# Routed experts: the gathered rows split first and turned by a transposing DMA, instead of turned by TensorE and split after

## The reference

```
H     = einsum('btd,od->bto', x, W) + adapter term        # c, the layer's output
sh    = sum_e gelu(c @ Wsh_up[e]) @ Wsh_down[e]           # 2 shared experts
probs = softmax(c @ W_router)                             # 16 experts, top 2
rt    = sum_e gate[:, e] * (gelu(c @ Wrt_up[e]) @ Wrt_down[e])
out   = x + sh + rt
```

## Time and profile before

| | us |
|---|---|
| median of three runs | 678.12 |
| span of the profiled execution | 642.9 |
| its own total | not given apart; median less span is 35.2 |
| PE busy, share of the span | 620.6, 97% |
| DVE, ACT, POOL busy | 427.3, 323.5, 169.7 |
| share of the 16 DMA engines by the SP queue / POOL queue | 40.7% / 20.9% |
| PE in the chain that ended last | 87% |
| L1405 (x transposes, 316 matmuls) in that chain | 5% |

### The profile page before, as it was taken

How to read it: one execution, slowest core, us unless ns; L and a number is a source line. 1 busy time by engine, 2 the same in 40 slices (tenths; PEclk the granted TensorE clock), 3 DMA queues, 4 the chain that set the end, 5 groups by cost and what they waited for, 6 DMA issues and landing times.

```text
span 642.9 us, 13313 instructions
## 1 busy us (share of the span) xinstructions
PE 620.6 (97%) x4116; PEld 430.5 (67%) x4117; DVE 427.3 (66%) x820; ACT 323.5 (50%) x487; POOL 169.7 (26%) x254
## 2 busy tenths in 40 slices
PE   4999999999999999989999999999999999999995
PEld 2566666666666677567777777777777777766662
DVE  2769989999888983355555555555555553688986
ACT  0256467676784522335555555555555554334340
POOL 0000000000001002233333333333333305777750
PEclk8999999999999999989999999999999999999999
DMA  6699974343235233385555555555555538999977
GB/s 277 258 377 422 421 274 164 130 163 132 105 116 203 102 131 126 112 303 164 163 160 160 158 158 163 155 162 161 161 161 163 163 114 296 342 311 388 397 278 245
DMA packets 49477, 135.62 MB, mean 211 GB/s; under 512 B 6000, under 2 KB 6000, under 8 KB 47024
## 3 DMA queue, kind: packets, MB, share of 16 engines
q1 hardware_dynamic: 38016, 97.86, 40.7%
q0 software_dynamic: 11440, 37.50, 20.9%
HBM read 86.31 MB, written 49.02 MB: 211 GB/s over the span
## 4 chain that ended last, share of the span: by engine, by line
PE 87%; DVE 6%; DMA 3%; ACT 1%; issue 1%; SPq 0%; POOL 0%; DVEq 0%; ACTq 0%; POOLq 0%
PE bank L1440 16%; PE bank L1421 16%; PE bank L1272 12%; PE bank L1349 11%; PE bank L1362 10%; PE bank L1405 5%; PE bank L1280 4%; PE bank L1297 4%; PE bank L1261 3%; PE bank L1430 3%; PE bank L1288 2%; PE bank L1335 1%; DMA region<-w_r 1%; DMA rtw<-x_rows 1%; DVE rtw L906 1%
## 5 line engine op out<-in xcount | busy, mean ns | idle before, releaser
L1149 DVE SCALAR_TENSOR_TENSOR region<-bank,scale,region 128x512 f16<-128x512 f32 x79 | 59.3, 750 | 114.3 <-ACT region L786 114.3
L1440 PE MATMUL bank<-rtw,tmp 128*128 x474 | 116.4, 382 | 2.8 <-DVE tmp L1157 2.8
L1421 PE MATMUL bank<-rtw,region 128*128 x948 | 116.7, 273 | 0.0
L1421 PEld LDWEIGHTS bank<-rtw,region 128*128 128x128 f16 x948 | 93.0, 98 | 10.3
L564 POOL DMA_INDIRECT region<-xc_dram,slot_idx x79 | 78.0, 988 | 61.3 <-POOL slot_idx L561 61.3
L1362 PE MATMUL bank<-shw,hid 128*128 128x512 f16 x384 | 86.2, 379 | 1.9 <-DVE rtw L1216 1.5
L1349 PE MATMUL bank<-act_in,shw 128*128 128x256 f16 x768 | 87.6, 273 | 0.1
L793 ACT ACTIVATE region<-bank,un_dn 128x512 f32<-128x512 f32 x79 | 54.3, 688 | 58.9 <-PE bank L1440 58.1
L1349 PEld LDWEIGHTS bank<-act_in,shw 128*128 128x128 f16 x768 | 75.0, 98 | 12.7 <-issue 0.6
L584 POOL DMA_INDIRECT rtw<-r_dram,pos x64 | 66.1, 1033 | 42.6 <-issue 37.1
L1440 PEld LDWEIGHTS bank<-rtw,tmp 128*128 128x128 f16 x474 | 46.6, 98 | 41.9 <-issue 4.2
(11 more groups left out here) (159 smaller groups left out, 829.4 us busy)
## 6 DMA issues: line engine op xcount, KB each, us to landing
r_dram<-region SPq DMA_DIRECT2D x79, 256.0 KB, 3.3
rtw<-rt_w SPq DMA_DIRECT2D x16, 1024.0 KB, 11.4
act_in<-xT SPq DMA_DIRECT2D x16, 512.0 KB, 4.3
xc_dram<-rows SPq DMA_DIRECT2D x16, 512.0 KB, 3.4
xcT_dram<-hid SPq DMA_DIRECT2D x16, 512.0 KB, 2.9
rtw<-x_rows SPq DMA_DIRECT2D x16, 512.0 KB, 5.5
rtw<-xcT_dram SPq DMA_DIRECT2D x10, 512.0 KB, 5.6
out<-rtw SPq DMA_DIRECT2D x9, 512.0 KB, 5.5
```

Source lines behind the costliest of these rows:

```text
L1149: nc.vector.scalar_tensor_tensor(xgT[s][:, 1], R_XT[s][:].rearrange("p (k t) -> p k t", k=HK), col(scale, C_ALL).bitcast(F32), xgT[s][:, 0 ...
L1421: last = mm(R_UP[s][:, 0:D], xgT[s][:, xp, k, :], rtw[:, bass.ds(e, 1), w0:w0 + D].rearrange("p a d -> p (a d)"), start=(k == 0 and n == 0 ...
L1440: last = mm(R_DN[s][:], midT[s][:, xp, m, :], rtw[:, bass.ds(e, 1), w0:w0 + H].rearrange("p a h -> p (a h)"), start=(m == 0 and n == 0), s ...
```

## The change

The x rows are split before they are turned. Each gathered tile stays in rows: ACT writes its high half and DVE its low half from `xg` into `xh[r]`, a [128, 2 x 512] float16 tile, and SP issues one `dma_start_transpose` that turns the 128 x 1024 numbers from SBUF into `xgT[r]`, [128, 8 x 128], also in SBUF. PE has no transposes of x any more, and the two PSUM banks of `R_XT` are unused in this stage. `xg`, `xh` and `xgT` become rings of three (`RING`), with `xh[2]` in the memory of `xam` and `xgT` and `rrow[1]` in that of `hid`. x is prepared three tiles ahead instead of two. All loops of the stage take six tiles (`TURN`), and what stands outside them is written out.

```diff
-        routed_bufs = carve([((H,), F32), ((2, HK, P), F16), ((H,), F32)] * 2)
-        xg, xgT, rrow = routed_bufs[0::3], routed_bufs[1::3], routed_bufs[2::3]
+        routed_bufs = carve([((H,), F32)] * RING + [((2, H), F16)] * 2 + [((H,), F32)])
+        xg = routed_bufs[0:RING]
+        xh = routed_bufs[RING:RING + 2] + [xam_both[:].bitcast(F16).rearrange("p (a h) -> p a h", a=2)]
...
+        def turn(i, m):
+            return TURN * i + m, m % RING, 2 * i + m // RING
@@ sync
+            def transpose_x(i, m, done=None):
+                j, r, n = turn(i, m)
+                if isinstance(i, int) and j < RING:
+                    sp.wait_ge(down_ready, NT * EARLY - NT if m < 2 else NT * EARLY)
+                sp.wait_ge(sorted_ready, 1)
+                if isinstance(i, int) and j < FIRST:
+                    sp.wait_ge(xh_first, j + 1)
+                else:
+                    sp.wait_ge(xh_ready, done)
+                sp.dma_start_transpose(xgT[r].rearrange("p a k t -> p (a k) t"),
+                                       xh[r].rearrange("p a h -> p (a h)")).then_inc(xgT_loaded[r], 16)
...
+            def move_step(i, m):
+                j = TURN * i + m
+                if not (isinstance(i, int) and j == 0):
+                    store_r(j - 1, (m - 1) % 2)
+                transpose_x(i + (m + RING) // TURN, (m + RING) % TURN, j)
@@ gpsimd, gather
-                if not first:
-                    pool.wait_ge(xgT_psum, j - 1)
+                if not first:
+                    pool.wait_ge(xh_ready, j - RING - FIRST + 1)
+                elif j >= RING:
+                    pool.wait_ge(xh_first, j - RING + 1)
@@ scalar
-            def r_high(j, s):
-                act.wait_ge(xgT_psum, j + 1)
-                nc.scalar.activation(xgT[s][:, 0], R_XT[s][:].rearrange("p (k t) -> p k t", k=HK), ACT.Copy,
-                                     scale=col(scale, C_ALL).bitcast(F32)).then_inc(xgT_half, 1)
+            def r_high(i, m):
+                j, r, n = turn(i, m)
+                act.wait_ge(xg_loaded[r], 16 * (n + 1))
+                if not (isinstance(i, int) and j < RING):
+                    act.wait_ge(xgT_loaded[r], 16 * n)
+                nc.scalar.activation(xh[r][:, 0], xg[r], ACT.Copy, scale=col(scale, C_ALL).bitcast(F32)).then_inc(xh_half, 1)
...
-                r_gelu(j, s)
-                r_high(j + 2, s)
+                r_gelu(j, m % 2)
+                r_high(i + (m + RING) // TURN, (m + RING) % TURN)
...
+            act.wait_ge(rrow_stored[1], 16 * NJ_2)
             high_hid(EARLY, 0)
@@ vector
-            def low_xgT(j, s):
-                dve.wait_ge(xgT_half, j + 1)
+            def low_x(i, m):
+                dve.wait_ge(xh_half, j + 1)
+                nc.vector.scalar_tensor_tensor(xh[r][:, 1], xg[r], col(scale, C_ALL).bitcast(F32), xh[r][:, 0],
+                                               ALU.mult, ALU.subtract).then_inc(xh_first if first else xh_ready, 1)
...
+            def split_step(i, m):
+                low_x(i + (m + RING) // TURN, (m + RING) % TURN)
+                split_midT(TURN * i + m, m % 2)
@@ tensor
-            def r_transpose_x(j, i, s, first=False):
-                pe.wait_ge(xg_loaded[s], 16 * (i + 1))
...
-                for k in range(HK):
-                    last = nc.tensor.transpose(R_XT[s][:, k * P:(k + 1) * P], xg[s][:, k * P:(k + 1) * P], ident[:])
...
-                pe.wait_ge(xgT_ready, j + 1)
+                pe.wait_ge(xgT_loaded[r], 16 * (n + 1))
...
+            def r_round(i, m, e, first=False):
+                j, s = TURN * i + m, m % 2
+                r_down(j, s, e[s], first)
+                r_transpose_mid(j + 1, 1 - s, first and m == 0)
+                r_up(i + (m + 2) // TURN, (m + 2) % TURN, e[2 + s])
```

More of the change, by code:

```diff
@@ L240, in col @@
             return v[:, n:n + 1]
-        slot_idx = [sb(f"slot_idx{s}", [P, 1], I32) for s in range(2)]
+        slot_idx = [sb(f"slot_idx{s}", [P, 1], I32) for s in range(RING)]
         bank = [ctx.enter_context(nc.psum_tensor(f"bank{i}", [P, 512], F32)) for i in range(8)]
@@ L1446, in _ @@
             pe.wait_ge(gelu_ready, EM * EARLY)
-            def r_round(i, first=False):
-                e = r_experts(i)
-                for s in range(2):
-                    j = 2 * i + s
-                    r_down(j, s, e[s], first)
-                    r_transpose_mid(j + 1, 1 - s, first and s == 0)
-                    r_up(j + 2, s, e[2 + s])
-                    r_transpose_x(j + 4, i + 2, s)
-            for s in range(2):
-                r_transpose_x(s, 0, s, first=True)
-                shared_down(2, 1, tiles=range(s, s + 1))
+            def r_round(i, m, e, first=False):
[3 more added lines that the diff above has]
+                r_up(i + (m + 2) // TURN, (m + 2) % TURN, e[2 + s])
@@ L1460, in _, with r_turn @@
+            def r_turn(i, first=False):
+                for m in range(0, TURN, 2):
+                    e = r_experts(RING * i + m // 2)
+                    r_round(i, m, e, first and m == 0)
+                    r_round(i, m + 1, e, first and m == 0)
+            shared_down(2, 1)
             e = r_experts(0)
             r_up(0, 0, e[0], first=True)
-            r_transpose_x(2, 1, 0)
             r_transpose_mid(0, 0, first=True)
-            r_up(1, 1, e[1], first=True)
-            r_transpose_x(3, 1, 1)
+            r_up(0, 1, e[1], first=True)
@@ L1466, in _ @@
             pe.wait_ge(shared_ready, NT * EARLY)
-            for i in range(2):
-                r_round(i, first=(i == 0))
-            with pe.Fori(2, NJ_2 - 2) as i:
-                r_round(i)
-            e = r_experts(NJ_2 - 2)
-            r_down(NJ - 5, 0, e[0])
-            r_transpose_mid(NJ - 4, 1)
-            r_up(NJ - 3, 0, e[2])
-            r_transpose_x(NJ - 1, NJ_2, 0)
-            r_down(NJ - 4, 1, e[1])
-            r_transpose_mid(NJ - 3, 0)
-            r_up(NJ - 2, 1, e[3])
+            r_turn(0, first=True)
@@ L1480, in _ @@
+            with pe.Fori(1, TURNS - 1) as i:
+                r_turn(i)
+            for m in range(0, TURN - 2, 2):
+                e = r_experts(RING * (TURNS - 1) + m // 2)
+                r_round(TURNS - 1, m, e)
+                r_round(TURNS - 1, m + 1, e)
             e = r_experts(NJ_2 - 1)
-            r_down(NJ - 3, 0, e[0])
-            r_transpose_mid(NJ - 2, 1)
-            r_up(NJ - 1, 0, e[2])
+            r_round(TURNS - 1, TURN - 2, e)
             r_down(NJ - 2, 1, e[1])
```

123 lines of the change are left out of this document (74 added, 49 removed).

## The result

| | before | after |
|---|---|---|
| median of the runs compared, us | 679.16 (4 runs) | 717.4 (4 runs) |
| profiled execution: its own time / span | not given / 642.9 | 720.14 / 718.3 |
| r_down(2) starts | 283.69 | 290.60 |
| 74 steps from there | 240.88, 3.26 each | 271.70, 3.67 each |
| last r_down to the end | 112.6 | 150.2 |

The changed kernel is 5.2% slower: ratio 1.052, 95% interval 1.0475 to 1.0565 (the two medians alone are 38.2 us, 5.6%, apart). The forecast was 669.5 with a range to 687; both were missed.

What follows compares the result with a forecast made beforehand. The prediction took PE, busy throughout the routed stage, as the bound, and the chain through ACT and DVE as the next. 678.12 - 13.1 (shorter steps) + 4.5 (start) = 669.5 us, range 660 to 687.

Steps and rivals of the forecast that it cites:

- Latency and queues: SP's transfer in mid-stage: issued 2.7 us after `r_down`, may take 5.0, taken as 4.3; the ring of three hides it.
- The latency rival: Mid-stage: the transpose lands late though the engines have room; 672 to 692 us, chance 0.14.
- T = 5.2: Mid-stage: transfer landing time in us from which lateness sets the step, three steps being 2.7 + T + 1.31.
- The engines' rate: Mid-stage rival: DMA engines set the step, 1.80 us plus the transpose, from 1.28; 670 to 698 and beyond, chance 0.23.
- the mark that was to tell the two rivals apart: With `r_up` waiting for DMA in mid-stage: DMA share near 1 means rate, under 0.9 means latency.
- My 0.9: DMA engines, per step: assumed transpose cost in us, the middle between store's 0.69 and gather's 1.11.
- what its packets look like: DMA engines: gather pays 1.6 times the store for the same bytes because of its packets; transpose pieces are smaller.
- The chain through ACT and DVE: Mid-stage: split behind low half of x sets the step, 3.08 us from links 3.18 and 2.98; gain 13.1, chance 0.56.
- the larger loop bodies: 0: Routed stage loops: no cost, since PE has 0.2 us of idle per step to hide a jump in.
- The start: Start of the routed stage: transposes queued around loads on SP cost +4.5 us, bounds +0.5 and +7.
- The first term: Stage start: transposes 0 and 1 ahead of chunk 5's x load delay `r_down(0)` by +1.0 us (0.2 to 1.5).
- 35.2 us around the span: Whole kernel: median 678.12 against profiled span 642.9; 35.2 us taken to lie outside the span, untouched by the change.

Runs made afterwards that it cites:

- second copy: The changed kernel run once more without edits, beside the kernel before on the same chip: 679.79 us against 644.93, ratio 1.0545.
- half a transfer: Changed kernel with its DMA turning only the high half of x, low half left out: 639.16 us, ratio 0.992 to the kernel before.
- the longer lead: Changed kernel with halves of x and transposing transfer prepared one tile further ahead, in the same three buffers: 644.33 us, ratio 0.9983 to the kernel before.
- the run that was to show it alone: Changed kernel with each gather held back by a wait for down products, one step more than intended: 776.62 us, ratio 1.2007 to the kernel before.
- the version with the longer lead and the split first: Changed kernel, x prepared one tile further ahead, DVE's split of mid before its low half of x: 636.74 us, ratio 0.9897 to kernel before.

## Why the prediction was wrong, point by point

**The step that failed is "Latency and queues".** It allowed the transfer 5.0 us and took 4.3 for its landing, "behind a store, and itself as large", and concluded that the ring hides it. The allowance was near: issued 404.96 - 402.11 = 2.85 after `r_down`, used 5.96 + 1.52 = 7.48 after it, by the starts in the timeline above, which leaves 4.6. The landing was not: 5.2 in the median and up to 8.1. One case from the second copy, all rows of one transfer:

```profile
394.87 1.29 SPq L453 DMA_TRANSPOSE hid<-region  x1
...
401.45 1.50 PE L1474 MATMUL bank<-rtw,hid 128*128 x12 [1.61 <-DMA hid<-region]
```

TensorE was ready at 401.45 - 1.61 = 399.84, 4.97 after the issue, and got the data after some 6.6. The margin of 0.7 us (5.0 allowed, 4.3 taken) was negative for the median transfer. The latency rival, with its decision point of T = 5.2, had 0.14 of the chance; it was the case. Its formula is for transfers that are all late alike; in truth 19 of 63 in mid-stage held TensorE up, by up to 4.3 us. From r_down(2) to 570 us of the second copy the waits for DMA are 31.2 us in 22, against 76 x (3.60 - 3.08) = 39.5 to be explained. Waits for the split and for "issue", 8.0 us, and the granted clock, 0.97 in mid-stage where it was 1.00, are in the remainder; how much each is worth is open.

**The engines' rate** was the rival that the number fits: 1.80 + 1.87 = 3.67, with the share near 1 that the prediction had named as its mark. It is not the cause, and the mark that was to tell the two rivals apart, near 1 for the rate and under 0.9 for latency, pointed to the wrong one: the share was 0.97. It adds up each packet from its start to its end, and at 1.10 in one version these must overlap on an engine. In the trace's packet records between 300 and 500 us the commonest 256-byte packet took 18 ns in every kernel with such transfers, and the mean was 27.3 in the changed kernel's second copy and 20.0 in the kernel before with a transfer more. 1024 packets by 18 ns over 16 engines are 1.15 us, under the 1.28 at which the rate would decide. My 0.9 was 0.25 too low for that, and harmless. The gather's 1.11 is such a mean too: its commonest packet, 4096 bytes in 159 ns, is per byte as fast as the store's, 2048 bytes in 84, and its packets are the larger ones, so the argument for this rival from "what its packets look like" was wrong. That a share of 0.97 is no full house is shown by 1.10 and 259 GB/s in 3.03-us steps. The Trainium skill's 261 GB/s ("DMA: Bandwidth & Descriptors", Latency and other measured facts) gives an estimate of 1.00 us; 1.15 is near it. The Trainium skill's "as fast as regular DMAs" ("Advanced Engine Details and Errata", X-Bar Transpose) would by the store's row be 0.69, and these runs don't agree.

**The chain through ACT and DVE** was right as a mechanism: steps in unlike pairs, the split behind the low half of x, and 2.88 once the split goes first. Its size was 0.1 a step too high, and that the means are 3.07 with half a transfer and 3.08 with the longer lead is in part luck. An undisturbed pair takes 5.97, not 6.16. The link from the start of one `r_down` to the end of `r_up` is 403.63 + 1.47 - 402.11 = 2.99, as foretold (2.98); the other, from the end of `r_up` to `r_down`, is 408.07 - 405.10 = 2.97, foretold as 3.18. Before the change the split began at 406.02, 0.79 after the low half's start and right behind the mid transposes; now it begins at 404.04, 0.67 after it. What brought the means back up was in part a term put at nothing, "the larger loop bodies: 0": the step in which a loop of six ends, 3.09 otherwise, is 3.1 to 3.3 in most cases with half a transfer and 3.4 to 3.6 with the longer lead. That the loop's jump does it is read from the place alone, no run took it out. Single long steps did the rest.

**The start**: +4.5 forecast, within bounds of 0.5 to 7; measured +6.9 (r_down(2) at 290.60). The mechanism, transfer 3 behind four loads, was right: issued at 279.04, it held `r_up` for 4.42 us until 288.07, and that `r_up`, at a granted clock of 0.50 between 288 and 290 us, took 2.74, 1.27 more than 1.47. The first term, the transfers in front of the load of x, was too small: `r_down(0)` came 1.96 later (277.44), not 1.0.

**35.2 us around the span** was wrong. A span is about 2 us short of its execution's time (718.3 and 720.14); span and median came from different executions. It shifted no difference: 38.2 measured, 6.9 + 30.8 = 37.7 by the rows.

**Why 5.2 and not 4.3?** Store, transposing DMA and gather are issued within 0.7 us and share the engines; the longer lead moves the transfer 0.45 us behind the next `r_down`, and its median landing is 4.3, though more is moved per us. There the three are still issued within 1.2 us (404.49, 405.21 and, last, 405.70). In the kernel before with one transfer more the gather goes first and store and transfer follow 1.0 and 1.4 us behind it, and the landing is 4.1. So it may be that the three together make it late, but it is not shown: the run that was to show it alone missed. How much of the cure is longer slack (7.1 in place of 4.6) and how much shorter landing is open. That the slack is too small for the landing, and not the engines for the bytes, is what the experiments show.

## What to carry to other kernels

When a transfer moves onto the critical ring, write down when it is issued, when it is used and what else is issued in the same microsecond, and compare the allowance with the worst landing under the load to come, not with the median at half of it. Before you believe that the DMA engines are full, issue the same transfers one step earlier in the buffers you have: if the time falls, it was latency. A busy share near 1 does not tell the two apart, GB/s against the best stretch does it better. And when a mean step comes out as foretold, look at the single steps before you call its mechanism right.

## What the runs showed of the hardware

- A transposing DMA of 128 x 1024 two-byte numbers, SBUF to SBUF, goes in packets of 256 bytes, commonly 18 ns each, and took 1.26 us (kernel before with one more) to 1.87 us (changed kernel) by the queue's share, in which packets that overlap count in full.
- It holds SP for 1.24 to 1.49 us in the median for 128 x 1024 and 1.22 to 1.28 for 128 x 512: nearly independent of size, against 0.33 for a store. Two a tile filled SP's time, 3.30 of a step of 3.33.
- The DMA share can exceed 1 (1.10, in the version with the longer lead and the split first).
- The same two kernels took 33 and 38 us more in their first runs than in the later ones (678 and 717 against 645 and 680), and among the later ones 645 held on four chips. What made the first ones longer is not shown.
